# Splitting the row maxima ahead of the transpose in a chain of four attention layers

## The reference, cut to what matters

```python
# each of the first three layers (scale and position bias differ)
scores = jnp.einsum('bhqd,bhkd->bhqk', q * scale, k)     # 8 heads, 1024 x 1024
attn = jax.nn.softmax(scores, axis=-1)
o = jnp.einsum('bhqk,bhkd->bhqd', attn, v)
```

## Time and profile before

| what | value |
|---|---|
| time, median of 3 runs | 510.47 us (510.2 to 511.23) |
| time of the profiled execution | 510.87 us |
| its span | 509.1 us |
| mean granted PE clock | 0.978 of full speed |
| busy: PE / DVE / ACT / POOL | 478.5 / 340.6 / 272.5 / 217.6 us |

### The profile page before, as it was taken

One profiled execution on the slowest core, in us unless ns is written; L12 is line 12 of the kernel. 1 busy time (PEld: TensorE's weight loads), 2 busy tenths in 40 slices (PEclk: granted clock), 3 DMA queues, 4 the chain that ended last, 5 costly groups with the idle time before them and its releaser, 6 DMA issues.

```text
span 509.1 us, 7000 instructions
## 1 busy us (share of the span) xinstructions
PE 478.5 (94%) x2264; PEld 240.1 (47%) x2264; DVE 340.6 (67%) x645; ACT 272.5 (54%) x520; POOL 217.6 (43%) x203
## 2 busy tenths in 40 slices
PE   8799999999899999999999989999999999989996
PEld 6444444443239565444444322664544444432463
DVE  7599888883264468987867522738988776722573
ACT  3228777777423324876757761131777765764032
POOL 8300031101000003899879981000699789987000
PEclk9979999999997999999999999998999999999999
DMA  5330442101000154488864540034457865452002
GB/s 146 55 56 22 136 67 35 21 5 21 1 0 1 26 116 106 86 197 172 185 118 88 94 91 6 1 91 105 93 115 155 178 120 102 84 102 46 0 1 82
DMA packets 18795, 39.85 MB, mean 78 GB/s; under 512 B 6478, under 2 KB 7638, under 8 KB 18632
## 3 DMA queue, kind: packets, MB, share of 16 engines
q1 hardware_dynamic: 13464, 23.39, 19.8%
q0 software_dynamic: 5152, 16.00, 17.1%
q10 hardware_dynamic: 144, 0.02, 0.0%
HBM read 4.76 MB, written 1.05 MB: 11 GB/s over the span
## 4 chain that ended last, share of the span: by engine, by line
PE 68%; DVE 10%; DMA 5%; SPq 4%; issue 4%; ACT 4%; POOL 3%; ACTq 0%; POOLq 0%; DVEq 0%
PE S L935 15%; PE PV L973 14%; PE S L962 13%; DVE max L705 6%; PE S L1083 4%; DMA k_stack<-kL 4%; POOL SUMS L492 3%; PE M L989 3%; PE PV L890 2%; SPq L301 2%; ACT E L556 2%; PE S L916 2%; PE M L916 2%; PE PV L916 2%; SPq L308 2%
## 5 line engine op out<-in xcount | busy, mean ns | idle before, releaser
L705 DVE TENSOR_REDUCE max<-S 128x1 f32<-128x512 f32 x384 | 239.0, 674 | 21.0 <-PE S L935 20.8
L556 ACT ACTIVATE E<-S 128x512 f32<-128x512 f32 x384 | 212.7, 604 | 71.5 <-PE S L962 67.3
L492 POOL TENSOR_TENSOR SUMS<-E 128x512 f32<-128x512 f32 x126 | 165.7, 1446 | 122.1 <-ACT E L556 122.0
L935 PE MATMUL S<-k_stack,q_stack 126*128 126x512 f32 x384 | 182.0, 484 | 9.4 <-DVE max L705 4.2
L962 PE MATMUL S<-q_stack,k_stack 128*128 128x512 f32 x384 | 155.3, 414 | 4.7 <-DMA q_stack<-mHL 2.3
L935 PEld LDWEIGHTS S<-k_stack,q_stack 126*128 126x128 f32 x384 | 74.0, 193 | 85.2 <-DVE max L705 60.2
L973 PE MATMUL PV<-E,V 128*32 128x512 f32 x768 | 95.4, 599 | 1.7 <-ACT pv_sb L563 1.7
L962 PEld LDWEIGHTS S<-q_stack,k_stack 128*128 128x128 f32 x384 | 72.5, 191 | 37.3 <-ACT E L556 22.1
L718 DVE TENSOR_TENSOR mHL<-S,mHL 4x128 fp32r<-4x128 f32 x48 | 13.3, 278 | 45.6 <-ACT mHL L545 45.6
L545 ACT ACTIVATE mHL<-S 4x128 fp32r<-4x128 f32 x48 | 12.6, 262 | 56.4 <-PE S L953 56.4
L973 PEld LDWEIGHTS PV<-E,V 128*32 128x32 f32 x768 | 20.0, 109 | 44.7 <-issue 26.9
(11 more groups left out here) (181 smaller groups left out, 334.4 us busy)
## 6 DMA issues: line engine op xcount, KB each, us to landing
SUMS<-SUMS POOLq DMA_DIRECT2D x30, 512.0 KB, 6.3
k_stack<-kH SPq DMA_DIRECT2D x32, 128.0 KB, 2.5
q_stack<-qH SPq DMA_DIRECT2D x40, 64.0 KB, 2.0
k_stack<-kL SPq DMA_DIRECT2D x16, 128.0 KB, 3.3
q_stack<-qH SPq DMA_DIRECT2D x16, 128.0 KB, 2.3
q_stack<-mHL SPq DMA_DIRECT2D x96, 2.0 KB
rec_sb<-den_sb SPq DMA_DIRECT2D x6, 256.0 KB
q_stack<-qL SPq DMA_DIRECT2D x20, 64.0 KB, 2.0
```

Source lines behind the costliest of these rows:

```text
L492: pool.tensor_tensor(SUMS[:, slot, :], E[:, E_PLAN[s][0], :], E[:, E_PLAN[s + 1][0], :], ALU.add).then_inc(sum_ready, 1)
L556: act.activation(E[:, slot, :], B[:, ring_of_scores(s) % B_RING, :], ACT.Exp, scale=1.0 if l == 0 else float(HEAD_DIM[l]) ** -0.5).then_in ...
L705: dve.tensor_reduce(max8[:, m % 2, r:r + 1], A[:, n % A_RING, :], AX.X, ALU.max, negate=True).then_inc(a_used, 1)
L935: pe.matmul(A[:, n % A_RING, :], q_stack[0:SHIFT_ROW, slot, q0:q0 + P], k_stack[0:SHIFT_ROW, slot, k0:k0 + HALF], start=True, stop=True).t ...
```

## The change

DVE now splits the maxima into high and low part while they are still columns on 128 partitions, so that one transpose brings eight rows instead of four. DVE's work on the transposed rows goes away, ACT copies eight rows in one instruction, and one DMA a unit brings both shift rows. The bank of `B` is free after ACT's copy.

```diff
-        negmax = sb("negmax", [P, 2, 4])
-        mHL = sb("mHL", [4, 2, 2, P], F32R)
+        mHL = sb("mHL", [8, 2, P], F32R)
+        maxHL = sb("maxHL", [P, 2, 3, 4], F32R)
...
-                for r in range(2):
-                    sp.wait_ge(rows_low if r else rows_high, m + 1)
-                    row = SHIFT_ROW + r
-                    sp.dma_start(q_stack[row:row + 1, slot_of(h), HALF * f:HALF * (f + 1)].bitcast(F32)
-                                 .rearrange("o (t c) -> o t c", t=4),
-                                 mHL[:, m % 2, r, :].bitcast(F32)).then_inc(shift_dma[m % 2], 16)
+                sp.wait_ge(rows_out, m + 1)
+                sp.dma_start(q_stack[SHIFT_ROW:P, slot_of(h), HALF * f:HALF * (f + 1)].bitcast(F32)
+                             .rearrange("r (t c) -> r t c", t=4),
+                             mHL[:, m % 2, :].bitcast(F32)).then_inc(shift_dma[m % 2], 16)
...
-                act.activation(mHL[:, m % 2, 0, :], B[0:4, ring_of_rows(j) % B_RING, 0:P], ACT.Copy).then_inc(rows_high, 1)
+                act.activation(mHL[:, m % 2, :], B[0:8, ring_of_rows(j) % B_RING, 0:P], ACT.Copy).then_inc(rows_out, 1)
...
-                    dve.tensor_reduce(negmax[:, m % 2, :], max8[:, m % 2, :].rearrange("p (t r) -> p t r", r=2), AX.X,
-                                      ALU.min).then_inc(negmax_ready, 1)
-
-            def low_rows(l, j):
-
-                m = UNITS_L * l + j
-                dve.wait_ge(rows_high, m + 1)
-                dve.tensor_tensor(mHL[:, m % 2, 1, :], B[0:4, ring_of_rows(j) % B_RING, 0:P],
-                                  mHL[:, m % 2, 0, :].bitcast(F32), ALU.subtract).then_inc(rows_low, 1)
+                    most, high, low = (maxHL[:, m % 2, part, :] for part in range(3))
+                    dve.tensor_reduce(most.bitcast(F32), max8[:, m % 2, :].rearrange("p (t r) -> p t r", r=2), AX.X,
+                                      ALU.max).then_inc(most_ready, 1)
+                    dve.wait_ge(most_ready, m + 1)
+                    dve.tensor_scalar(high, most.bitcast(F32), -1.0, None, ALU.mult).then_inc(max_split, 1)
+                    dve.wait_ge(max_split, 2 * m + 1)
+                    dve.tensor_reduce(low.bitcast(F32), maxHL[:, m % 2, 0:2, :].bitcast(F32).rearrange("p a t -> p t a"), AX.X, ALU.add,
+                                      negate=True).then_inc(max_split, 1)
...
-                    if s in ROWS_AT:
-                        low_rows(l, ROWS_AT[s])
...
             def transpose_max(l, j):
                 m = UNITS_L * l + j
-                pe.wait_ge(negmax_ready, m + 1)
+                pe.wait_ge(max_split, 2 * (m + 1))
                 ring_free(l, ring_of_rows(j))
-                pe.transpose(B[0:4, ring_of_rows(j) % B_RING, 0:P], negmax[:, m % 2, :], ident[:, :]).then_inc(rows_done, 1)
+                pe.transpose(B[0:8, ring_of_rows(j) % B_RING, 0:P], maxHL[:, m % 2, 1:3, :].rearrange("p a t -> p (a t)").bitcast(F32),
+                             ident[:, :]).then_inc(rows_done, 1)
```

More of the change, by code:

```diff
@@ L190, in attention_chain @@
         a_done, a_used = sem("a_done"), sem("a_used")
-        negmax_ready, rows_done = sem("negmax_ready"), sem("rows_done")
-        rows_high, rows_low = sem("rows_high"), sem("rows_low")
+        most_ready, rows_done = sem("most_ready"), sem("rows_done")
+        max_split, rows_out = sem("max_split"), sem("rows_out")
         shift_dma = [sem(f"shift_dma{i}") for i in range(2)]
@@ L537, in project_out, with shift_out @@
                 act.activation(high, src, ACT.Identity, bias=bias, scale=scale).then_inc(high_ready, 1)
-            def high_rows(l, j):
+            def shift_out(l, j):
                 m = UNITS_L * l + j
@@ L543, in high_rows @@
                 if m >= 2:
-                    act.wait_ge(shift_dma[m % 2], 32 * (m // 2))
-                act.activation(mHL[:, m % 2, 0, :], B[0:4, ring_of_rows(j) % B_RING, 0:P], ACT.Copy).then_inc(rows_high, 1)
+                    act.wait_ge(shift_dma[m % 2], 16 * (m // 2))
+                act.activation(mHL[:, m % 2, :], B[0:8, ring_of_rows(j) % B_RING, 0:P], ACT.Copy).then_inc(rows_out, 1)
             def probabilities(l, s):
@@ L599, in _ @@
                     project_out(l, n)
-                high_rows(l, 0)
+                shift_out(l, 0)
                 for s in range(STEPS):
                     if s in ROWS_AT:
-                        high_rows(l, ROWS_AT[s])
+                        shift_out(l, ROWS_AT[s])
                     probabilities(l, s)
@@ L703, in maxima @@
                 if r == 0 and m >= 2:
-                    dve.wait_ge(negmax_ready, m - 1)
-                dve.tensor_reduce(max8[:, m % 2, r:r + 1], A[:, n % A_RING, :], AX.X, ALU.max,
-                                  negate=True).then_inc(a_used, 1)
+                    dve.wait_ge(max_split, 2 * (m - 1))
+                dve.tensor_reduce(max8[:, m % 2, r:r + 1], A[:, n % A_RING, :], AX.X, ALU.max).then_inc(a_used, 1)
                 if r == TILES - 1:
@@ L944, in ring_free @@
                 if kind == "rows":
-                    pe.wait_ge(rows_low, UNITS_L * l + at + 1)
+                    pe.wait_ge(rows_out, UNITS_L * l + at + 1)
                 else:
@@ L959, in scores @@
                 if t == 0:
-                    pe.wait_ge(shift_dma[m % 2], 32 * (m // 2 + 1))
+                    pe.wait_ge(shift_dma[m % 2], 16 * (m // 2 + 1))
                 ring_free(l, ring_of_scores(s))
```

## The result

The changed kernel takes 558.66 us (median of 4 runs, 557.09 to 559.42), the kernel before 510.85 in the same series (4 runs, 510.2 to 512.83). The ratio is 1.0925, with a 95% interval of 1.0886 to 1.0964: 9% slower. The profiled execution took 558.92 (its span 557.2), against 510.87 before (span 509.1).

What follows compares the result with a forecast made beforehand. PE was taken to bound the attention loops, with 0.65 us a unit owed to DVE's late restart; early units were DVE-bound. Layer terms of -2.5, -2.35 and -1.55 gave -6.4, about 504 us, range 499.5 to 515.

Steps and rivals of the forecast that it cites:

- The tensor_scalar beside POOL: Layers 1 and 2: multiplication waits to the running add's end, 0 to 1.3 us, taken 0.8; early units +0.5 a layer.
- The third rival: Layers 1 and 2: DVE shut out for whole strings of POOL's adds; about 534 us, 520 if half; chance 0.20.
- The upper bound of 3.5 us: Multiplication beside POOL, layers 1 and 2: waits for the whole string of adds, up to 4.06 us less 0.6.
- the range of 515: Whole kernel: 499.5 to 515 us, leaving out the case of DVE shut out for whole strings.
- The second rival: Layers 1 and 2: DVE's asking locks to an add's start, wait 1.3 us each time; about 509 to 515; chance 0.13.
- L718 goes: Attention units: maxima restart at T + 0.57 instead of T + 0.82 (T: transpose start), 0.25 us less; layer 0 gains 2.5.
- Two small DVE instructions: DVE ahead of PE's transpose: next maximum 0.38 us later, free in units with L973; early units net + 0.3 a layer.
- ACT's copy of eight rows: ACT's copy of the transposed rows: eight rows for four priced at 0, bounds 0 to 0.27 us more.
- One DMA for two: SP's queue: 0.64 us freed a unit; load stalls of 1.23 and 0.71 gone; reciprocals' wait 0.8 and 0.5 less.
- The sum: Whole kernel: layer 0 -2.5, layer 1 -2.35, layer 2 -1.55, together -6.4 us; median about 504.

Runs made afterwards that it cites:

- the spare tile: The kernel before plus one tensor_scalar of 128x4 between two halves of an extra SBUF tile behind negmax in every unit, its result unused: 555.68 us, ratio 1.0871.

## Why the prediction was wrong

**The step that failed** is "The tensor_scalar beside POOL", and in it the value taken: "If DVE gets its turn at the end of the add that is running, it waits 0 to 1.3, 0.8 in the middle." In 22 of the 26 units of layers 1 and 2 in which it meets adds it doesn't get its turn there. When the next add has begun before the running one ends, it waits for the whole string: 3.33 us in the unit shown, 38.9 us over the 16 of layer 1, of which the first three, which meet no add, take 0.17 each. The third rival said this, at 0.20. The cause is shown by runs from both sides: the multiplication alone makes the loss (555.68), its exchange for a reduction takes it away (503.47), and a gap of 0.17 us between the adds takes most of it away (513.44, one run).

The row I leaned on against that rival was the earlier trace rows, the copy that "did get in before the string had ended". It stands beside `memset`s that end and start afresh every 0.15 us, and I had noted the difference; but the same row also showed the copy passed over at the end of the running `memset`, which the forecast needed it not to be. Of the two readings I took the milder one. The upper bound of 3.5 us was nearly right (the steady units take 3.0 to 4.14): it was in the text, but the range of 515 left it out.

By the Trainium skill (SBUF — State Buffer, "Who interferes with whom"), a DVE instruction that can enter a 2-port mode and GpSimd exclude each other for the whole instruction, and `tensor_reduce` never enters one. The traces agree on both (1670 ns and 161 ns). They also show DVE staying out over the ends of POOL's instructions, where the next one has begun before the end.

**The third rival's size.** It gave 534, the kernel takes 558.66. Its place was right, and its period (8.25) nearly: 8.5 and 8.7. Three terms were too small. Behind the standing PE ran at its lower clock for a while (8.0 us more busy in layer 1), which the rival didn't have at all. It gave the waits to ten units a layer, four of them with only 0.5; there are waits of PE in 13 of 16. And it left the first units uncharged once POOL adds, where DVE has no cover: the fourth and fifth of layer 1 take 0.90 and 2.67, while the forecast's own sum had 0.5 for a layer's early units together. The second rival's sum doesn't come out as written either: with its "5 x 0.9 more" taken per layer, as its other terms are, it gives about 517.5 and not 509 to 515.

**What was right**, read from the kernel with the reduction, in which the failed step is taken out:
- *L718 goes.* Forecast: transposes 6.2 apart in layer 0, restart at T + 0.57. Measured: 66.99 - 60.78 = 6.21 from unit to unit; in layer 1 the transpose starts at 225.17 and maxima go on at 225.72, T + 0.55. Layer 0 gave 2.1 us for the 2.5 forecast, in the changed kernel too.
- *Two small DVE instructions.* Forecast 0.19 apart; they start at 60.78, 60.98 and 61.17, 0.20 apart, and are covered.
- *ACT's copy of eight rows.* Priced at 0. Its median is 266 ns with eight rows in the changed kernel and 266 ns with four before.
- *One DMA for two.* The stall of 1.23 at the earlier trace rows is gone, as forecast; that of 0.71 is gone in one profiled run and 0.51 in the other (405.34). POOL's wait for the spread reciprocals went from 1.22 to nothing in one profiled run and to 0.15 in the other. I had given the DMAs 3.2 us (2.0 in layer 1 and 1.2 in layer 2; the 0.3 beside them was L718's); they are worth 4.85.
- *The sum.* Without the multiplication's waits (0.5 in the five plain units and 0.5 in the early ones, in two layers: 2.0 us) the terms come to -8.4; measured are -7.6 and -7.7. But the split of it was wrong: with two DMAs only 2.85 us are left of all that L718's going should bring (about 5 by my terms). The waits with two DMAs suggest a reason: PE waits for loads and shift rows again, 8.2 us where it was 6.2 before the change (3.9 + 2.3). My sum had the two terms independent; by this reading they aren't. That the term for L718 was simply too large in layers 1 and 2 isn't ruled out.

Which of the late transfers ate which part of the gain stays open. So does whether the first of the two DMAs, which in the kernel before could leave ahead of the second, mattered there: both versions with the reduction have one copy, and both DMAs wait for it.

## What to carry to other kernels

Before a small DVE instruction is put beside GpSimd work, lay the two timelines over each other and ask of what kind it is and where its source lies: on 128x4 between two SBUF tiles, `tensor_scalar` and `scalar_tensor_tensor` waited for GpSimd (means of 1670 and 1629 ns), `tensor_reduce` (161) did not, and neither did the seven `tensor_scalar` with a source in PSUM that fell inside an add (0.15 us at most). Price such a wait by the length of the string that GpSimd runs without a gap, not by one instruction, and let the range reach to that bound where a row already shows an instruction passed over. A shut-out stands in the trace as a long duration with no releaser, so an instruction whose maximum is 24 times its minimum (4141 and 169 ns) on equal shapes is a sign to look for.

## What the runs showed that I had not expected

- An ending add of POOL lets DVE in with 0.17 us until the next (longest multiplication 1.88 us), and in 22 units of the changed kernel, where the next add's record begins 0.3 us before the end, it doesn't (4.14 us). In two units with an overlap of 0.04 it does.
- The longest ones of the changed kernel, 4.14 us at 254.36 and at 438.65, begin 0.09 us ahead of the string's first add, while POOL issues a DMA (253.84, 0.88 us). With the spare tile one that began 0.08 ahead of an add, with no DMA issue there, took 0.16 (249.93). So the DMA issue seems to belong to the string; no run was made for this alone.
- Four columns are enough: the length of the DVE instruction doesn't protect it, nor does it matter whether anyone waits for its result (555.68 with nobody waiting).
- PE's standing costs twice: the granted clock fell to 0.52 for over 3 us behind a wait of 1.75 us. Over the program its mean was 0.940 for 0.978, but not all of that comes from here: in layer 0, where POOL adds nothing, it was at the lower level for 13.65 us (from 22.63) for 6.83 before (from 29.0).
- In the kernel with the reduction POOL's strings in layer 1 fill each 6.20 us (223.27 to 229.47) with 5.29 of adds and the issue of a DMA between. PE's pace there is 6.21. Whoever makes PE faster in these layers is likely to meet POOL next; that wasn't tried.
